# A two-layer decoder whose cross attentions are computed in row halves and column tiles of TensorE, with the softmax sums folded by GpSimd and the normalisation done by ScalarE

## The reference, cut to what matters

```
q = split_heads(x @ Wq + bq);  k, v = split_heads(ctx @ Wk + bk), split_heads(ctx @ Wv + bv)
score = einsum('bhqd,bhkd->bhqk', q, k) / 4          # layer 1: + mask * -1e9
o = einsum('bhqk,bhkd->bhqd', softmax(score), v)     # 16 heads, 64 keys each
x = layernorm(x + (o merged @ Wo + bo))              # mean and variance over 256, eps 1e-5
```

## Time and profile before

| | us |
|---|---|
| median of 3 runs | 1582.75 |
| lowest and highest | 1580.85, 1583.4 |
| span of the profiled execution | 1580.5 |
| first to last maximum (L792), layer 0 | 195.2 to 295.1 |
| first to last maximum (L792), layer 1 | 1096.6 to 1208.3 |

### The profile page before, as it was taken

The page is one execution under the profiler, slowest core; times in us unless marked ns, Lnnn a source line. Parts: engine busy times, 40 slices in busy tenths (PEclk is TensorE's granted clock), DMA queues, the critical chain, the costliest instruction groups (busy, mean ns, idle before and its releaser), DMA issues. The chain is left out here.

```text
span 1580.5 us, 24800 instructions
## 1 busy us (share of the span) xinstructions
PE 1324.1 (84%) x7871; PEld 905.2 (57%) x7872; DVE 821.7 (52%) x1539; ACT 655.7 (41%) x1921; POOL 508.1 (32%) x592
## 2 busy tenths in 40 slices
PE   7888599744889999999999999984998529999980
PEld 3544378522656667666666666653776425666650
DVE  1288578777535545553445555643776752222215
ACT  3498344311356655565555556531432101222212
POOL 0055312235144522322533222000122324555535
PEclk9999699855899999999999999996998559999995
DMA  9000000000111001000001001008000101111105
GB/s 296 1 1 1 0 1 1 1 0 0 41 24 32 15 14 23 7 15 21 21 20 22 15 1 41 1 1 319 1 1 0 61 6 41 43 43 46 46 34 159
DMA packets 36131, 55.97 MB, mean 35 GB/s; under 512 B 6528, under 2 KB 27392, under 8 KB 36032
## 3 DMA queue, kind: packets, MB, share of 16 engines
q1 hardware_dynamic: 32288, 44.47, 9.5%
q0 software_dynamic: 3744, 10.23, 2.0%
HBM read 34.90 MB, written 9.31 MB: 28 GB/s over the span
## 5 line engine op out<-in xcount | busy, mean ns | idle before, releaser
L1666 DVE TENSOR_REDUCE ga_neg_top<-ps 128x1 f32<-128x128 f32 (+7 forms) x256 | 182.1, 753 | 182.3 <-PE ps L1383 181.5
L1392 PE MATMUL ps<-ident,ga_e 128*128 128x128 f32 x1152 | 188.5, 282 | 7.0 <-ACT ga_e_tr L1525 4.5
L1516 ACT ACTIVATE ga_e<-ps,ga_neg_top 128x128 f32<-128x128 f32 (+7 forms) x256 | 188.2, 743 | 5.9 <-DVE ga_neg_top L1666 5.2
L1408 PE MATMUL ps<-ga_e_tr,ga_v 128*64 128x256 f32 x1152 | 165.1, 395 | 6.8 <-ACT ga_att L1533 6.7
L1525 ACT COPY ga_e_tr<-ps 128x512 f32<-128x512 f32 (+3 forms) x192 | 91.9, 479 | 186.3 <-PE ps L1392 185.0
L1392 PEld LDWEIGHTS ps<-ident,ga_e 128*128 128x128 f32 x1152 | 122.7, 141 | 79.3 <-issue 64.1
L2100 PE MATMUL ps<-ex_gate_up,ex_scratch 128*128 x312 | 143.3, 603 | 0.6 <-ACT ex_scratch L2133 0.6
L1674 DVE COPY ga_e_tr<-ps 128x128 f32<-128x128 f32 (+3 forms) x192 | 101.9, 552 | 50.5 <-PE ps L1392 49.2
L188 POOL TENSOR_TENSOR tail_rstd<-tail_var_eps,neg_half 128x1 f32<-128x1 f32 x80 | 52.6, 658 | 234.3 <-DVE tail_var_eps L216 234.3
L195 POOL COPY x_nat<-tail_xn 128x256 f32<-128x256 f32 (+1 forms) x80 | 31.7, 396 | 230.2 <-DVE tail_xn L226 230.2
L2155 DVE TENSOR_TENSOR ex_scratch<-ex_scratch,ps 128x512 f32<-128x512 f32 x39 | 26.8, 687 | 136.9 <-ACT ex_scratch L2128 136.9
(11 more groups left out here) (292 smaller groups left out, 2761.7 us busy)
## 6 DMA issues: line engine op xcount, KB each, us to landing
ga_q_swapped<-ga_q_raw SPq DMA_DIRECT2D x64, 128.0 KB, 2.3
ex_gate_up<-in_ex_gate_up SPq DMA_DIRECT2D x1, 8192.0 KB, 23.7
ex_down<-in_ex_down SPq DMA_DIRECT2D x1, 4096.0 KB, 36.1
x_tr<-in_x_tr SPq DMA_DIRECT2D x4, 512.0 KB, 7.3
x_nat<-in_x SPq DMA_DIRECT2D x1, 2048.0 KB, 11.7
ga_k_swapped<-ga_k_raw SPq DMA_DIRECT2D x16, 128.0 KB, 2.3
xn_rows<-x_tr SPq DMA_DIRECT2D x8, 256.0 KB, 2.1
x_tr<-choice_rows SPq DMA_DIRECT2D x8, 256.0 KB, 5.9
```

The costliest lines, as they stand in the source:

```text
L1392: last = nc.tensor.transpose(ps_tr[n % 2][:, (kb - k0) * P:(kb - k0 + 1) * P], e[half][t % 2][:, kb * P:(kb + 1) * P], core.ident[:])
L1408: last = nc.tensor.matmul(ps_att[half * HD:(half + 1) * HD, :], v[:, v_slot(b, kb), kv * HD:(kv + 1) * HD], e_tr[g % 2][:, kb, half, :], s ...
L1516: nc.scalar.activation(e[half][t % 2][:, 0:blocks(t) * P], ps_scores(t, half), ACT.Exp, bias=neg_top[t % 2][:, half:half + 1], accum_out=s ...
L1666: nc.vector.tensor_reduce(neg_top[t % 2][:, half:half + 1], ps_scores(t, half), AX.X, ALU.max, negate=True).then_inc(top_ready, 1)
```

## The change

It rewrites the steady part of `stage_cross_attention` and leaves all other stages and `Tail` as they are.
- The loop is unrolled: 21 steps written out (`tiles_of`), the same five lags.
- Scores: `k_diag` now holds four masked copies a half (256 columns), in which the upper and the lower 64 rows serve different heads. A product takes 64 rows of q and of `k_diag` and gives four heads; the upper 64 rows write one PSUM bank, the lower 64 the other. There are four such products a tile in place of two of 512 columns. In layer 1 the mask goes first, over both banks, before q is waited for.
- The product with V is turned round: `v_pairs` is the stationary side (32 columns a pair), `e_tr` moves (128 columns), and the result comes out transposed, each pair on its own 32 partitions. Its transposes on TensorE (L658) are gone. It moves one step later, to u3.
- The reciprocals are spread to 128x256 by GpSimd (`recip_wide`), turned by TensorE, copied by ScalarE (`recip_tr`), and VectorE multiplies with them straight into `mixed_tr`.
- Sums: GpSimd adds the halves of the 64 exponentials of each head, then the halves of that; VectorE sums the 16 that are left.
- Norm: GpSimd computes variance plus eps, the inverse root and the offset; ScalarE writes `z * rstd + offset` straight into `x_nat`, which TensorE then turns.
- The copy of the transposed weights is in two halves, and the order of each queue is new. `e` still has one buffer, and so has each PSUM area.

```diff
@@ stage_cross_attention @@
     mask_parts = core.sb(ctx, f"{pre}_mask_parts", [P, 2, SEQ_TILES, CTX], F32R)
...
+ps_y = core.ps_y[:, 0:D]
+ps_recip = core.ps_ct[:, 0:D]
+ps_xt = core.ps_ct[:, D:2 * D]
+def tiles_of(step):
+    return [step - lag if 0 <= step - lag < TILES else None for lag in range(LAGS + 1)]
...
+        by_head = e[:].rearrange("p (m k) -> p m k", k=CTX)
+        for step in range(TILES + LAGS):
+            t, u1, u2, u3, u4, u5 = tiles_of(step)
+            if u3 is not None:
+                pool.wait_ge(recip_ready, u3 + 1)
+                need(pool, recip_tr_ready, u3)
+                nc.gpsimd.tensor_copy(recip_wide[:].rearrange("p (h d) -> p h d", d=DEPTH),
+                                      recip[:].unsqueeze(2).to_broadcast([P, HEADS, DEPTH])).then_inc(wide_ready, 1)
             if u4 is not None:
+                need(pool, z_ready, u4)
+                nc.gpsimd.tensor_tensor(resid[:], x_nat[:, u4, :], bo_row[:], ALU.add).then_inc(resid_ready, 1)
+            if u2 is not None:
+                pool.wait_ge(e_ready, u2 + 1)
+                need(pool, total_ready, u2)
+                nc.gpsimd.tensor_tensor(folded[:], by_head[:, :, 0:CTX // 2], by_head[:, :, CTX // 2:CTX], ALU.add).then_inc(half_folded, 1)
+                pool.wait_ge(half_folded, u2 + 1)
+                nc.gpsimd.tensor_tensor(folded[:, :, 0:CTX // 4], folded[:, :, 0:CTX // 4], folded[:, :, CTX // 4:CTX // 2],
+                                        ALU.add).then_inc(folded_ready, 1)
             if u4 is not None:
+                pool.wait_ge(var_ready, u4 + 1)
+                need(pool, xn_ready, u4)
+                nc.gpsimd.tensor_scalar(var_eps[:], mv[:, 1:2], LN_EPS, None, ALU.add).then_inc(eps_added, 1)
+                pool.wait_ge(eps_added, u4 + 1)
+                nc.gpsimd.tensor_tensor(rstd[:], var_eps[:], core.neg_half[:], ALU.pow).then_inc(rstd_ready, 1)
+                pool.wait_ge(rstd_ready, u4 + 1)
+                nc.gpsimd.tensor_scalar(offset[:], mv[:, 0:1], rstd[:, 0:1], -1.0, ALU.mult, ALU.mult).then_inc(offset_ready, 1)
...
+        for step in range(TILES + LAGS):
+            t, u1, u2, u3, u4, u5 = tiles_of(step)
+            if u1 is not None:
+                need(pe, shifted_ready, u1)
+                if masked:
+                    for r in range(2):
+                        for part in range(2):
+                            nc.tensor.matmul(core.ps_s[:, r * BANK:(r + 1) * BANK], ident_r[:],
+                                             mask_parts[:, part, u1 % SEQ_TILES, :].unsqueeze(1).to_broadcast([P, HALF_HEADS, CTX]),
+                                             start=(part == 0), stop=False)
+                pe.wait_ge(q_copied, u1 + 1)
+                for h in range(KD):
+                    for r in range(2):
+                        rows = slice(r * ROWS, (r + 1) * ROWS)
+                        s = core.ps_s[:, r * BANK + h * D:r * BANK + (h + 1) * D]
+                        last = nc.tensor.matmul(s, q_tr[rows, h, :], k_diag[rows, u1 // SEQ_TILES, h, :, :],
+                                                start=not masked, stop=(h == KD - 1 or not masked))
+                        if h == KD - 1:
+                            last.then_inc(s_ready, 1)
+            if u3 is not None:
+                pe.wait_ge(e_tr_copied, 2 * (u3 + 1))
+                need(pe, mixed_ready, u3)
+                for h in range(KD):
+                    for c in range(P // LANE):
+                        r, i = divmod(c, QUARTER // 2)
+                        j = r * PAIRS // 2 + h * QUARTER // 2 + i
+                        last = nc.tensor.matmul(core.ps_c[c * LANE:(c + 1) * LANE, h * P:(h + 1) * P],
+                                                v_pairs[:, u3 // SEQ_TILES, h * P + c * LANE:h * P + (c + 1) * LANE], e_tr[:, j, :],
+                                                start=True, stop=True)
+                        if h == KD - 1:
+                            last.then_inc(mix_ready, 1)
+                pe.wait_ge(wide_ready, u3 + 1)
+                need(pe, recip_tr_copied, u3)
+                need(pe, xt_copied, u3 - 2 if not masked else 0)
+                for h in range(KD):
+                    last = nc.tensor.transpose(ps_recip[:, h * P:(h + 1) * P],
+                                               recip_wide[:, h * P:(h + 1) * P], core.ident[:])
+                last.then_inc(recip_tr_ready, 1)
+            if u4 is not None:
+                pe.wait_ge(mixed_ready, u4 + 1)
+                need(pe, z_ready, u4)
+                for k in range(KD):
+                    last = nc.tensor.matmul(ps_y, mixed_tr[:, k, :], wo[:, k, :], start=(k == 0), stop=(k == KD - 1))
+                last.then_inc(y_ready, 1)
+            if u5 is not None and not masked:
+                pe.wait_ge(xn_ready, u5 + 1)
+                need(pe, xt_copied, u5)
                 if u3 is not None:
+                    pe.wait_ge(recip_tr_copied, u3 + 1)
                 for k in range(KD):
+                    last = nc.tensor.transpose(ps_xt[:, k * P:(k + 1) * P], x_nat[:, u5, k * P:(k + 1) * P], core.ident[:])
+                last.then_inc(xt_ready, 1)
             if t is not None:
                 need(pe, q_copied, t)
                 for h in range(KD):
                     for k in range(KD):
                         last = nc.tensor.matmul(core.ps_q[:, h * P:(h + 1) * P], wq[:, k, h * P:(h + 1) * P],
+                                                x_tr[:, k, t * P:(t + 1) * P], start=(k == 0), stop=(k == KD - 1))
                 last.then_inc(q_ready, 1)
+            if u2 is not None:
+                pe.wait_ge(e_ready, u2 + 1)
+                for half in range(2):
+                    need(pe, e_tr_copied, 2 * u2 - 1 + half)
+                    for j in range(half * PAIRS // 2, (half + 1) * PAIRS // 2):
+                        last = nc.tensor.transpose(core.ps_e[:, j * P:(j + 1) * P], e[:, j * P:(j + 1) * P], core.ident[:])
+                    last.then_inc(e_tr_ready, 1)
...
+        for step in range(TILES + LAGS):
+            t, u1, u2, u3, u4, u5 = tiles_of(step)
+            if u2 is not None:
+                act.wait_ge(shifted_ready, u2 + 1)
+                need(act, e_tr_ready, 2 * u2)
+                need(act, half_folded, u2)
+                nc.scalar.activation(e[:], shifted[:], ACT.Exp, scale=SCORE_SCALE).then_inc(e_ready, 1)
+            if u5 is not None:
+                act.wait_ge(offset_ready, u5 + 1)
+                act.wait_ge(z_ready, u5 + 1)
+                nc.scalar.activation(x_nat[:, u5, :], z[:], ACT.Identity, bias=offset[:, 0:1],
+                                     scale=rstd[:, 0:1]).then_inc(xn_ready, 1)
             if u3 is not None:
+                act.wait_ge(recip_tr_ready, u3 + 1)
+                need(act, mixed_ready, u3)
+                nc.scalar.copy(recip_tr[:], ps_recip).then_inc(recip_tr_copied, 1)
+            if u5 is not None and not masked:
+                act.wait_ge(xt_ready, u5 + 1)
+                nc.scalar.copy(x_tr[:, :, u5 * P:(u5 + 1) * P], ps_xt.rearrange("p (k t) -> p k t", k=KD)).then_inc(xt_copied, 1)
             if t is not None:
                 act.wait_ge(q_ready, t + 1)
+                need(act, s_ready, 2 * t)
                 for h in range(KD):
                     last = nc.scalar.activation(q_tr[:, h, :], core.ps_q[:, h * P:(h + 1) * P], ACT.Identity,
                                                 bias=bq[:, h:h + 1])
                 last.then_inc(q_copied, 1)
+            if u2 is not None:
+                for half in range(2):
+                    pairs = slice(half * PAIRS // 2, (half + 1) * PAIRS // 2)
+                    act.wait_ge(e_tr_ready, 2 * u2 + half + 1)
+                    need(act, mix_ready, P // LANE * u2)
+                    nc.scalar.copy(e_tr[:, pairs, :], core.ps_e[:, half * BANK:(half + 1) * BANK]
+                                   .rearrange("p (j q) -> p j q", q=P)).then_inc(e_tr_copied, 1)
...
+        nc.vector.tensor_tensor(quarter_mask[:], head_mask[:, 0:QUARTER], head_mask[:, QUARTER:HALF_HEADS], ALU.add).then_inc(quarter_ready, 1)
+        dve.wait_ge(quarter_ready, 1)
         dve.wait_ge(k_copied, 1)
         for b in range(BATCH):
             for h in range(KD):
                 last = nc.vector.tensor_tensor(
-                    k_diag[:, b, h, :, :], k_tr[:, h, b * CTX:(b + 1) * CTX].unsqueeze(1).to_broadcast([P, HALF_HEADS, CTX]),
-                    head_mask[:].unsqueeze(2).to_broadcast([P, HALF_HEADS, CTX]), ALU.mult)
+                    k_diag[:, b, h, :, :], k_tr[:, h, b * CTX:(b + 1) * CTX].unsqueeze(1).to_broadcast([P, QUARTER, CTX]),
+                    quarter_mask[:].unsqueeze(2).to_broadcast([P, QUARTER, CTX]), ALU.mult)
...
+        in_rows, in_halves = ("p (r h i) -> p r h i", "p (h r i) -> p r h i")
+        for step in range(TILES + LAGS):
+            t, u1, u2, u3, u4, u5 = tiles_of(step)
             if u1 is not None:
```

(36 more changed lines are left out.)

120 lines of the change are left out of this document (20 added, 100 removed).

## The result

| | before | after |
|---|---|---|
| median of the runs, us | 1581.8 (4 runs, the three shown above among them) | 1529.37 (4 runs, 1528.72 to 1529.64) |
| span of the profiled execution, us | 1580.5 | 1527.0 |
| ratio to before | | 0.9669, 95% interval 0.9655 to 0.9683 |

What follows compares the result with a forecast made beforehand. TensorE was taken to bound both layers: 15 steps at 5.22 for 6.66 us (layer 0) and 5.92 for 7.45 (layer 1) save 21.6 + 23.0, less 2.4 at the ends, 42.2 off: 1540 us, range 1526 to 1563.

Steps and rivals of the forecast that it cites:

- Product with V, 0.75: TensorE's sixteen passes on four column tiles take 0.75 us a step, between pairs (1.01) and four at once (0.50).
- a rival at 0.16: Four column tiles run at once: product with V 0.50 us, GpSimd ring holds layer 0 at 5.12, 1535 us; chance 0.16.
- Scores, 1.01: TensorE's eight score passes of 256 columns in row halves take 1.01 us a step, bounds 0.86 and 1.72.
- Changes of shape, 0.31: Two switches a step on TensorE, row halves to column tiles and column tiles to full, cost 0.31 us together.
- Sum: TensorE's parts per step: 3.15 + 1.01 + 0.75 + 0.31 = 5.22 us in layer 0, 5.92 in layer 1.
- The ring through GpSimd: Waits over two steps through GpSimd's spread, TensorE, VectorE and GpSimd's norm: 10.2 us, 5.12 a step, hidden in layer 0.
- The ring of ScalarE: ScalarE's copies, exponential and normalisation, then TensorE's turn and next queries: 5.1 us a step, barely under 5.22.
- GpSimd's and VectorE's prices: Work a tile: GpSimd 4.16 us (upper bound 6.15 if strided folds cost twice), VectorE 4.65, both below TensorE's 5.22.
- All fifteen intervals at the steady pace: Savings between maxima taken as 15 full steps: 21.6 us in layer 0, 23.0 in layer 1.
- Start, -1.4 a layer: Cheaper first scores at half clock shorten the start of each cross attention by 1.4 us, bounds 0 and 3.
- End, +2.6 a layer: From last maximum to last copy, the last tile's path takes 2.6 us more a layer, bounds -1 and +4.
- lone loads: Rival: column-tile weight loads stand alone, so product with V costs 2.18 us; 1583.5, no change; chance 0.04.

## Why the prediction was right or wrong

*The bound.* Right but for 0.13 us a step of layer 0, where the ring below sets the pace. TensorE's microseconds paid, and the granted clock held between the maxima.

*Product with V, 0.75.* This step failed. The run with one column tile and the cut windows show four tiles at once, 0.58. I had given this to a rival at 0.16, and its mechanism is the one that took place. My reason against it, that a float32 product is two passes on the same tile, is no hindrance: passes of other tiles run beside it in both orders that were run.

*Scores, 1.01.* Right: 1.06, and 1.88 with the halves undone.

*Changes of shape, 0.31.* Too dear. Unchanged parts and scores, forecast at 3.15 + 1.01, measure 3.22 + 1.06, so at most 0.12 is left there for the changes. One is seen alone: full-height scores take 1.88 ahead of the column tiles and took 1.72 ahead of the projection before, 0.16 as forecast for one change. The turns of `e` take 0.97 in layer 0 where they took 0.87 before, but they do so ahead of full-height scores too, so that isn't a change of shape; its cause is open.

*Sum.* 4.86 for 5.22, and 5.57 for 5.92. The mask: turns, mask and scores are 0.79 + 1.11 + 1.07 in layer 1 and 0.97 + 1.06 in layer 0, 0.94 for the forecast 0.92.

*The ring through GpSimd.* Right in place, and its cover did fail because TensorE was quicker: two steps take 9.98 us against the forecast 10.2 of the ring. The rival had it at 5.12 in each step; it is 4.86 and 5.12 in turn, since only their sum is bound. Moved out of the ring, the turn gave 0.09 a step. The ring of ScalarE, laid end to end at 5.1, never showed: steps of 4.86 pass.

*GpSimd's and VectorE's prices.* Right. The folds measure 1.27 and 0.74 on strided views, forecast 1.26 and 0.73; a tile costs GpSimd 4.19 (forecast 4.16) and VectorE 4.53 (4.65).

*All fifteen intervals at the steady pace.* A simplification that cost 5.8 us. While the pipeline fills, TensorE lacks the later parts: the first three intervals are 3.75 in layer 0 and 4.87 in layer 1. So 15 steady intervals of 4.99 would be 74.85 and not 71.15, and 83.6 not 81.5. With the steady step's 3.4 and 5.2 this accounts, to 0.1, for the 14.3 us that the two stretches gave beyond the forecast. Part of it is luck: with the first steps at half clock, as in five of the other traces, the stretch of layer 0 is some 1.8 us longer.

*Start, -1.4 a layer.* It is -2.9, for two reasons that the run with full-height scores shows. In layer 0 that kernel starts as the one before (12.6 us), and the row-halved ones take 10.8 to 11.2 us in nine traces: 1.5 to 1.9 us off, with the scores at half clock in both. The profiled execution has 9.8 because its first scores ran at full clock (3.44 us before, 1.07 after, about 2.0 in the others); that part is luck. In layer 1 the full-height kernel takes 14.9 us, so the row halves are 1.2 of the 2.9, and the other 1.7 came with the rest of the change, most likely with the mask, which now goes ahead of the wait for q; I had left that out. The 1.35 us ahead of layer 0 are within what that stretch moves by from trace to trace.

*End, +2.6 a layer.* Mis-sized: +6.9 and +5.3, beyond the upper bound of 4. The one part is the 1.37 and 1.0 from the last instruction to the next stage, of which fifteen semaphores are 1.06 each by the run that added as many. The other is the order of TensorE's queue (0.4 and 0.75 us come back with the turns moved), the half clock that took 1.1 and 1.6 us in this execution, and single buffers of `z` and the residual (another 1.2). Together that is 4.1 of the 6.9 and 4.6 of the 5.3; what is left, 2.8 and 0.7, would be the longer way of the last tile, which the forecast had at 2.6, if these parts add; no run shows it by itself.

In all: 42.2 forecast, plus 14.3 between the maxima, plus 3.0 at the starts, plus 1.0 elsewhere, less 7.0 at the ends, is 53.5. The number was 10.6 too high in a range that held it. The direction was right, and so was the mechanism, TensorE's own work made cheaper by tiles side by side, except for how many tiles run at once; there the rival given 0.16, with 1535, was closer. Errors of opposite sign, the fill and the ends above all, hid each other in part.

*The rule of the skill.* The changed kernel's sixteen loads and sixteen passes lie within 0.58 us, and on one tile, where they can't be side by side, within 1.87, less than the 2.18 that I worked out for lone loads. The Trainium skill, "TensorE: Matmul & The Clock Gate", section on packing small matmuls, lets a load overlap running matmuls only for another row group; these share one, so the trace disagrees. The same section gives 2.38 times for three column tiles; the 3.2 times for four here point the same way.

## What to carry to other kernels

Small stationary blocks on different column tiles run beside each other, four at a time in both orders that were run, so turning a product round so that its narrow side is stationary can cut it to a third (1.70 to 0.58 us here) and save the transposes of its result, though here the reciprocals had to be turned in their place. When the bound engine gets cheaper, look at each wait at the head of its queue in two places: in the steady step, where it may cost nothing, and at the end of the stage, where the same wait holds all that is behind it. Price the fill and the end of a pipeline by themselves, with every single buffer and every semaphore counted: here they came out 5.8 us better and 7.0 us worse than forecast, in a gain of 53. And before a stretch of a few microseconds in one profile is explained, look at the same stretch in the traces of kernels that share its code: here starts and ends moved by more than 1 us with the granted clock alone.

## What the runs showed of the hardware that I had not expected

- Four column tiles of 32 columns at once: sixteen float32 passes of 128 columns in 0.58 us, 1.87 on one tile, 0.60 when issued tile by tile.
- Semaphores of a stage cost time at its end, even unused: fifteen more made the gap to the next stage 1.06 us longer in both layers, 0.07 each.
- The granted clock after a short wait differs between executions of the same code: the first scores of layer 0 take 1.07 us from start to start in one trace and 2.00 in others, and the end of layer 0 takes 20.5 or 19.3.
- A step that alternates (4.86, 5.12) was here the sign of a ring over two steps that is longer than two of the bound engine's; an average hides it, the starts of one instruction in a row show it.
